# Opening of a linear-attention layer: sums of sizes in place of peaks, another order of the preparations, masks ahead of the bias

## The reference

```python
x = x + attn(layernorm(x))          # qkv = n @ W_attn + b_attn; q, k -> elu(.) + 1
x = x + ffn(layernorm(x))           # x and weight clipped, rounded to e4m3, product in fp16, + bias
def step(carry, inp):               # attention, one token at a time, per head
    kv = kv + kt[..., :, None] * vt[..., None, :]
    ksum = ksum + kt
    num = einsum('bhi,bhij->bhj', qt, kv)
    den = einsum('bhi,bhi->bh', qt, ksum)[..., None] + EPS
    y = num / den                   # then y @ W_proj + b_proj
def _layernorm(x, eps=1e-05):
    return (x - mean) / sqrt(var + eps)
```

## Time and profile before

| what | value |
|---|---|
| median of 3 runs | 1105.98 us (1104.98 to 1107.2) |
| the profiled execution's own time | 1102.66 us |
| its span in the profile | 1100.8 us |
| TensorE, matmuls | 1025.5 us busy, 93% of the span |
| VectorE | 827.4 us, 75% |
| GpSimd | 718.8 us, 65% |
| ScalarE | 568.9 us, 52% |
| granted TensorE clock, mean | 0.992 |

### The profile page before, as it was taken

The page is one execution under the profiler, slowest core; times in us unless marked ns, Lnnn a source line. Parts: engine busy times, 40 slices in busy tenths (PEclk is TensorE's granted clock), DMA queues, the critical chain, the costliest instruction groups (busy, mean ns, idle before and its releaser), DMA issues.

```text
span 1100.8 us, 25183 instructions
## 1 busy us (share of the span) xinstructions
PE 1025.5 (93%) x10112; PEld 557.2 (51%) x10112; DVE 827.4 (75%) x1447; ACT 568.9 (52%) x937; POOL 718.8 (65%) x718
## 2 busy tenths in 40 slices
PE   5877999999999999999999999999999999999976
PEld 2334555555555555555554555555455555555543
DVE  7888767777786867878686786777778777775655
ACT  4454463654646456364555546465554745546343
POOL 5346788576677757667576767758666775864444
PEclk9989999999999999999999999999999999999999
DMA  9201312213131231312213141221313123130011
GB/s 315 39 11 29 78 39 64 59 48 74 42 71 49 59 68 35 87 41 58 63 40 78 45 78 43 60 68 41 73 49 69 43 66 61 40 63 26 25 30 58
DMA packets 121924, 65.59 MB, mean 60 GB/s; under 512 B 102480, under 2 KB 102480, under 8 KB 121808
## 3 DMA queue, kind: packets, MB, share of 16 engines
q1 hardware_dynamic: 121808, 63.99, 23.4%
HBM read 22.81 MB, written 16.78 MB: 36 GB/s over the span
## 4 chain that ended last, share of the span: by engine, by line
PE 41%; POOL 30%; DVE 16%; ACT 6%; issue 6%; DMA 1%; SPq 0%; POOLq 0%; DVEq 0%; ACTq 0%
PE R L219 32%; POOL sm L948 9%; POOL st L916 6%; PE Y L219 5%; POOL xs L964 5%; POOL xn L918 4%; POOL xs L933 4%; DVE st L605 3%; POOL x L918 3%; DVE xs L717 3%; ACT rel L446 2%; PE S L311 2%; ACT qkv L443 2%; DVE state L700 1%; DVE cum L650 1%
## 5 line engine op out<-in xcount | busy, mean ns | idle before, releaser
L219 PE MATMUL R<-xt,wh 128*128 128x512 f16 x960 | 288.1, 382 | 18.2 <-ACT rel L446 17.7
L628 DVE SCALAR_TENSOR_TENSOR qkv<-qkv,rel 128x512 f32<-128x512 f32 x128 | 119.5, 934 | 133.7 <-ACT rel L446 131.9
L916 POOL TENSOR_TENSOR st<-st,half 128x1 f32<-128x1 f32 x128 | 93.4, 730 | 149.1 <-DVE st L610 143.2
L948 POOL TENSOR_SCALAR_AFFINE_SELECT sm<-sm 128x512 f32<-128x512 f32 x184 | 183.4, 1024 | 7.3 <-ACT sm L431 7.3
L219 PE MATMUL R<-xt,wl 128*128 128x512 f16 x480 | 183.0, 381 | 0.0
L219 PEld LDWEIGHTS R<-xt,wh 128*128 128x128 f16 x960 | 89.3, 98 | 124.1 <-ACT rel L446 21.3
L219 PE MATMUL R<-wh,xt 128*128 128x512 f16 x480 | 150.3, 379 | 0.0
L943 POOL TENSOR_TENSOR cum<-cum,qkv 128x512 f32<-128x512 f32 x64 | 84.8, 1325 | 97.6 <-DVE cum L648 50.4
L955 POOL TENSOR_TENSOR yl<-y,yh 128x512 f16<-128x512 f32 x64 | 74.8, 1169 | 97.1 <-ACT yh L431 96.2
L443 ACT ACTIVATE qkv<-R,bqk,wm 128x512 f32<-128x512 f32 x128 | 99.2, 775 | 63.9 <-PE R L219 63.3
L431 ACT ACTIVATE yh<-y 128x512 f16<-128x512 f32 x64 | 40.3, 630 | 155.7 <-DVE y L710 155.7
(11 more groups left out here) (108 smaller groups left out, 1878.8 us busy)
## 6 DMA issues: line engine op xcount, KB each, us to landing
xs<-in_L_attn_x SPq DMA_DIRECT2D x64, 256.0 KB, 2.9
out<-xs SPq DMA_DIRECT2D x64, 256.0 KB, 2.0
qkv<-in_L_attn_W_attn SPq DMA_DIRECT2D x3, 1024.0 KB, 7.9
xs<-in_L_attn_W_proj SPq DMA_DIRECT2D x1, 1024.0 KB, 8.9
rden<-in_L_ffn_weight SPq DMA_DIRECT2D x1, 1024.0 KB, 12.4
x2t<-x2b SPq DMA_TRANSPOSE x62, 2.4
xt<-xnhl SPq DMA_TRANSPOSE x60, 3.2
bv<-in_L_attn_b_attn SPq DMA_DIRECT2D x1, 256.0 KB, 8.1
```

The costliest lines, as they stand in the source:

```text
L219: return e.matmul(out, a, b, start=start, stop=stop, skip_group_check=True)
L628: e.scalar_tensor_tensor(qkv[j % 2][:, i, :], qkv[j % 2][:, i, :], 1.0, rel[:, (u - 1) % 2, :], ALU.min, ALU.add).then_inc(s_phi, 1)
L916: e.tensor_tensor(row[:, 10:11], row[:, 9:10], half[:, :], ALU.pow).then_inc(s_rs, 1)
L948: e.affine_select(out=four(sm[:, h, :]), in_=four(sm[:, h, :]), compare_op=ALU.is_ge, fill=0.0, base=0, pattern=[[0, 4], [1, P]], channel_ ...
```

## The change

Four things change. First, the bounds for the scales of the q, k and projection weights are no longer peaks made by VectorE but sums of absolute values made by ScalarE in one instruction over 128 x 2048 with an accumulated output (`attn_size`, `proj_size`); only the v weight keeps its peak (`v_peak`). The scale of the three is half as large, 2^-14 in place of 2^-13. Second, the lists of the opening are put in another order on all engines, and the fp8 pieces of the feed-forward weight move to the space of `o16` and `x2b`, with one more wait on ScalarE. Third, the negated mean is no longer made; GpSimd subtracts the mean. Fourth, GpSimd masks the scores before it adds the projection's bias, and not behind it.

```diff
-        w_lo = x2[:, 0, :].bitcast(F8)...
-        w_hi = x2[:, 1, :].bitcast(F8)...
+        w_lo = o16[:, :, :]...bitcast(F8)...
+        w_hi = x2b[:, :, :]...bitcast(F8)...
 # TensorE
             def most(i):
-                pe.wait_ge(s_peak, i + 1)
+                if i == 2:
+                    pe.wait_ge(s_peak, 1)
+                else:
+                    pe.wait_ge(s_size, min(i, 2) + 1)
             def k_tokens(n):
                 if n >= 2:
                     pe.wait_ge(s_y, n - 1)
+                elif n:
+                    pe.wait_ge(s_ktok, 1)
-            for m in range(3):
+            for m in range(4):
                 t1(m)
             most(0)
-            t1(3)
             for i in range(12):
                 proj_qkv(0, i)
-                if i in (0, 2):
-                    most(1 if i == 0 else 2)
+                if i in (0, 4, 10):
+                    most((0, 4, 10).index(i) + 1)
             k_tokens(0)
             den(0)
-            most(3)
             for n in range(NT + 2):
...
-                    if c == 0:
+                    if c == 0 and j:
                         lend_out(j, (0, 1))
...
                     ahead(j + 1, 3 * c + 2)
+                    if n == 0:
+                        lend_out(0, (0, 1))
                     if c == 0:
                         lend_out(j, (2, 3))
 # ScalarE
+            def attn_size(i):
+                cols = slice(i * D, (i + 1) * D)
+                act.wait_ge(s_wa[i], 16)
+                e.activation(wl[:, :, cols].bitcast(BF16), raw[:, :, cols], ACT.Abs,
+                             accum_out=wm[:, 7 * i:7 * i + 1]).then_inc(s_size, 1)
+            def proj_size():
+                act.wait_ge(s_wp, 16)
+                e.activation(wpl[:, :, :].bitcast(BF16), raw_p, ACT.Abs, accum_out=wm[:, 21:22]).then_inc(s_size, 1)
...
+            t1(0)
+            t1(1)
+            attn_size(0)
+            t1(2)
+            t1(3)
             attn_weight(0)
             attn_weight(1)
+            attn_size(1)
             phi(0, 0)
             attn_weight(2)
             attn_weight(3)
             phi(0, 1)
             phi(0, 2)
-            attn_weight(4)
             ln1_parts(4)
             phi(0, 3)
-            attn_weight(5)
             ln1_parts(5)
             phi(0, 4)
+            attn_weight(4)
             ln1_parts(6)
             phi(0, 5)
+            attn_weight(5)
             ln1_parts(7)
             phi(0, 6)
+            proj_size()
             phi(0, 7)
...          # in the loop, tile 0: proj_weight() after k_tokens(1), lend_out(0, (0, 1))
...          # after ahead(1, 2), ffn_half() after values(0); t2(n) for n < 2 waits for s_wfd at 5
 # VectorE
-                e.tensor_scalar(row[:, 8:9], row[:, 6:7], -1.0, None, ALU.mult)
...
             for m in range(4):
                 ln1(m)
-            attn_peak(0)
             t1_parts(0)
             t1_parts(1)
+            parts_less()
             scale(0)
             t1_parts(2)
             t1_parts(3)
             attn_weight(0)
             attn_weight(1)
-            attn_peak(1)
             ln1(4)
             scale(1)
+            ln1(5)
             attn_weight(2)
             phi(0, 0)
-            ln1(5)
             attn_weight(3)
             phi(0, 1)
-            attn_peak(2)
+            ln1(6)
             phi(0, 2)
+            v_peak()
+            ln1_parts(4)
+            ln1(7)
+            phi(0, 3)
+            ln1_parts(5)
             scale(2)
-            ...
+            phi(0, 4)
+            denominators(0, 0)
             attn_weight(4)
-            ...
             ln1_parts(6)
             phi(0, 5)
+            denominators(0, 1)
+            attn_weight(5)
+            ln1_parts(7)
             v_scale()
-            ln1_parts(7)
             phi(0, 6)
+            denominators(0, 2)
             phi(0, 7)
-            for g in range(4):
-                denominators(0, g)
-                v_out(0, g)
-            parts_less()
-            proj_peak()
+            denominators(0, 3)
+            for t in range(4):
+                v_out(0, t)
+            ln1(8)
+            proj_scale()
             invert(0)
             den_rest(0)
-            proj_scale()
-            den_third(0)
...          # den_third(0) after scores(0); ffn_low() after update(0), ffn_high() after update(1)
 # GpSimd
-                return e.tensor_scalar(dst, src, row[:, 8:9], row[:, 10:11], ALU.add, ALU.mult)...
+                return e.tensor_scalar(dst, src, row[:, 6:7], row[:, 10:11], ALU.subtract, ALU.mult)...
...
                     if n + 8 < NT:
                         ln1(n + 8)
-                        add_bp(n + 8)
                     scores(n)
                     after(j + 1, 3 * c)
+                    if n + 8 < NT:
+                        add_bp(n + 8)
 # SyncE
-                if n == 0:
+                if n == 1:
                     sp.wait_ge(s_wfd, 5)
                     for f in range(4):
                         e.dma_start(wft[:, :, f * P:(f + 1) * P], w_b[:, f, :], transpose=True)...
```

More of the change, by code:

```diff
@@ L164, in build @@
         s_xth, s_wh, s_relu, s_whi = sem("xth"), sem("wh"), sem("relu"), sem("whi")
-        s_xhi, s_ktok, s_dene = sem("xhi"), sem("ktok"), sem("dene")
+        s_xhi, s_ktok, s_dene, s_size = sem("xhi"), sem("ktok"), sem("dene"), sem("size")
         s_top16, s_mid16, s_rden = sem("top16"), sem("mid16"), sem("rden")
@@ L523, in t2 @@
                     act.wait_ge(s_x2t[i], 16 * (n // 2))
+                else:
+                    act.wait_ge(s_wfd, 5)
                 copy(x2b[:, i, :], x28[:, :]).then_inc(s_x2b, 1)
@@ L543, in ahead, with t1 @@
                         den(j)
-            for m in range(4):
+            def t1(m):
                 act.wait_ge(s_t1, m + 1)
                 copy(xt0[:, 0:4, m * P:(m + 1) * P], four(bank["t1", m][:, :])).then_inc(s_xth, 1)
+            t1(0)
[3 more added lines that the diff above has]
+            t1(3)
             attn_weight(0)
             attn_weight(1)
+            attn_size(1)
             phi(0, 0)
@@ L576, in _ @@
                         ln1_parts(n + 8)
-                    if n == 0:
-                        proj_weight()
                     ahead(j + 1, 3 * c + 1)
-                    if c == 0:
+                    if c == 0 and j:
                         lend_out(j, (0, 1))
@@ L583, in _ @@
                     k_tokens(n + 1)
+                if n == 0:
+                    proj_weight()
                 if n >= 2:
@@ L587, in _ @@
                     ahead(j + 1, 3 * c + 2)
+                    if n == 0:
+                        lend_out(0, (0, 1))
                     if c == 0:
                         lend_out(j, (2, 3))
-                    if n == 0:
-                        ffn_half()
                     if c == 3 and j + 1 < NB:
@@ L594, in _ @@
                     values(n)
+                if n == 0:
+                    ffn_half()
                 if n >= 2:
@@ L754, in scale @@
                 dve.wait_ge(s_range, 3 * i + 2)
-                e.tensor_scalar(wm[:, at + 4:at + 5], wm[:, at + 3:at + 4], 2.0 ** -13, None,
+                e.tensor_scalar(wm[:, at + 4:at + 5], wm[:, at + 3:at + 4], 2.0 ** (-13 if i == 2 else -14), None,
                                 ALU.mult).then_inc(s_range, 1)
@@ L758, in scale, with v_peak @@
                 e.reciprocal(wm[:, at + 5:at + 6], wm[:, at + 4:at + 5]).then_inc(s_up, 1)
-            def attn_peak(i):
-                dve.wait_ge(s_wa[i], 16)
-                peak(raw[:, :, i * D:(i + 1) * D], wm[:, 7 * i:7 * i + 1], AX.XY).then_inc(s_peak, 1)
+            def v_peak():
+                dve.wait_ge(s_wa[2], 16)
+                peak(raw[:, :, 2 * D:], wm[:, 14:15], AX.XY).then_inc(s_peak, 1)
             def t1_parts(m):
@@ L791, in v_scale @@
                 e.tensor_scalar(bv[:, :], bv[:, :], wm[:, 32:33], None, ALU.mult).then_inc(s_bv, 1)
-            def proj_peak():
-                dve.wait_ge(s_wp, 16)
-                peak(raw_p, wm[:, 21:22], AX.XY).then_inc(s_peak, 1)
             def proj_scale():
@@ L878, in _ @@
                 if n < NT:
-                    if n + 8 < NT:
+                    if n and n + 8 < NT:
                         ln1(n + 8)
                     scores(n)
+                    if n == 0:
+                        den_third(0)
                     ahead(j + 1, 3 * c)
@@ L886, in _ @@
                         ln1_parts(n + 8)
-                    if n == 0:
-                        ffn_low()
                     ahead(j + 1, 3 * c + 1)
@@ L897, in _ @@
                     ahead(j + 1, 3 * c + 2)
-                    if n == 0:
-                        ffn_high()
                     values(n)
                     update(n)
+                    if n == 0:
+                        ffn_low()
+                    if n == 1:
+                        ffn_high()
                     if c == 3 and j + 1 < NB:
@@ L917, in norm @@
```

(2 more changed lines are left out.)

11 lines of the change are left out of this document (2 added, 9 removed).

## The result

The changed kernel takes 1234.48 us (1233.57 to 1235.28, four runs) against 1106.09 us; the ratio is 1.116 with a 95% interval of 1.1141 to 1.118. It is 128.4 us slower; 1080 was forecast, with a range to 1091. The profiled execution took 1233.57 us, its span is 1231.7 us.

A forecast was written before the change was run, and what follows sets the result against it. TensorE was taken as the bound, so only its 75.3 us of idle time could shrink. Opening 9.8, masks 14.9 and norms 1.3 sum to 26.0 us, from 1105.98 to 1080 us; range 1073 to 1091.

The forecast's parts named there:

- the part on the norms: All 128 norms: one small VectorE instruction less each, GpSimd's norm still one instruction, nothing lost there; 1.3 us gained.
- the slower rival: Middle: masks now beside VectorE's two-input work cost 1.36 us a tile, half on TensorE's path; 1118 us, chance 0.03.
- Masks: Middle: masks ahead of the bias add end 1.5 us earlier, removing TensorE's 26 waits for `sm`; 14.9 us, bounds 5 to 14.9.
- The doubt that another partner would take them back: Middle: the next late partner replaces the masks' waits, 5 us of 14.9 left; 1090 us, chance 0.10.
- Norms without negated means: VectorE's statistics: 0.07 us less per norm, shortening 14 waits for `rel` and the last four norms; 1.3 us, bounds 0 to 2.5.
- Opening: Start to the scores of tile 3: reordered preparations bring these from 119.81 to 110.0; 9.8 us gained, bounds 4 to 13.
- The walk: Opening followed on TensorE step by step: gains of 3.8, 6.8 and 13.0 us, partly given back in tile 2, leaving 9.8.
- rival (a): Opening gives little: `ffn_high` keeps VectorE late, or the sixth low weight's wait lowers the clock; 1086 to 1088 us, chance 0.17.
- the third term: The 1.3 us gained by no longer making the negated mean for the norms on VectorE.
- The sum over 128x2048: Opening, ScalarE: absolute values with a sum in one instruction, taken as 2.0 us, between 1.8 and 4.8.
- rival (c): Opening, ScalarE: table loads on both sides of each sum, six of 1.28 us, some 4 on the path; 1084 us, chance 0.06.
- so I count no slow stretch: Opening, new 2.9 us stall before the first product of v: clock expected to hold, as behind an earlier 2.76 us wait.

The follow-up runs named there:

- the run with the pieces moved: Changed kernel with the old add-and-multiply norm, and the five pieces of the feed-forward weight's rounding moved into idle time in tile 0: 1068.71 us, ratio 0.9663.
- the run with the forms: Kernel before, with another pair of operations in GpSimd's norms by tile modulo 8 (most tiles compute other values): 1151.5 us.
- the reordered kernel: Changed kernel with old norm and feed-forward pieces moved into idle time, plus parts_less, scale(2), late weights and running sums reordered in the opening: 1066.17 us, ratio 0.9639.

## Why the prediction was wrong

**The step that failed** is in the part on the norms: "Nothing is lost on GpSimd, whose norm stays one instruction." The count was right, but no row showed that the duration would stay. The trace of before shows add+mult on 128x512 at 767 ns and no subtract in that form. I gave the new pair the price of the old one and set no bounds on it from both sides. The trace of before held a warning: a two-input add over the same shape takes 1.28 us on average there (the second bias add), so GpSimd's time depends on more than size. Subtract+mult costs 2.08 us, 128 x 1.31 = 168 us of GpSimd, and on the path of TensorE 155.9 us (1234.48 - 1078.58). No rival named the norm; the slower rival (masks shut out by VectorE) named the wrong mechanism.

**Masks.** Right in direction and cause: no wait for `sm` from 100 to 1050 us was left with the masks moved alone or with the old norm; in the changed kernel 5.7 us in 14 are, behind the slow norms. The term was 14.9 us and measured 26.3, in the main because the table of waits counts from the modelled end of the last matmul. The doubt that another partner would take them back was unfounded, as were the 38 us of the slower rival.

**Norms without negated means.** Priced at 1.3 us for the VectorE instruction less; the kernel that adds the mean is 4.7 us under the one with the old norm (one run against a median of four). Only VectorE's own 0.07 us was counted, and not what came with it: the wait of 1.28 us in every second block fell to 0.72.

**Opening.** 9.8 us forecast, 3.4 measured alone and 0.6 beside the masks (1079.21 - 1078.58, inside the scatter; in the traces tile 4 starts within 0.6 us of where it started without the new opening). The walk was right for GpSimd's `part` holding `scale(0)` (forecast 14.1, 13.97 in the run with the old norm), for the first product (16.4 and 16.30), for the stall that goes and for the wait of 4.5 us in `lend_out` (5.6 in three). Too small were the wait for the sixth low weight (2.9, measured 4.55, with the clock at 0.66 from 45 to 50, where I had it hold) and that of tile 2 (4, measured 6.59, with clock 0.51 behind it). This is rival (a), which the run with the pieces moved bears out. For opening and masks together 24.7 us were forecast and 26.9 measured: a gain of the opening that was put too high and one of the masks that was put too low nearly cancel. With the third term and a norm of the old price, 26.0 were forecast and 31.7 measured (1105.52 - 1073.86, the run that adds the mean). That the total without the slow pair came out near 1080 is luck.

**The sum over 128x2048** was priced at 2.0 us. The groups of ScalarE after (count | busy, mean ns):

```profile
L458 ACT ACTIVATE wl<-qkv 128x2048 bf16<-128x2048 f32 x2 | 3.8, 1898 | 0.0
...
L436 ACT ACT_TABLE_LOAD x1 | 1.3, 1283 | 0.8 <-PEq L1135 0.8
...
L458 ACT ACTIVATION_READ_ACCUMULATOR wl<-qkv 128x1 f32 x2 | 0.4, 190 | 0.0
```

It is 1.90 us and 0.19 for reading the accumulator. There is one table load in the whole trace, at the start as before, so rival (c) is out. The Trainium skill (ScalarE: Activation LUTs, Table sets) says that abs stands in every set; the trace agrees for the one set that this kernel loads, whose exp runs beside it.

## What to carry to other kernels

A rewrite that saves an instruction by another pair of operations is a new instruction: until a trace shows that pair on that engine and shape, its price is open, and where it stands twice in a chain that already ends waits, each microsecond more can be two in each tile (here 1.31 more was 2.8). Time it alone first. Read TensorE's waits as a lower bound where short matmuls overlap, and take their price from the distance between two fixed points of a tile in a kernel with and without them.

## What the runs showed of the hardware

- GpSimd's `tensor_scalar` with two scalars over 128x512 fp32, in the run with the forms: 0.77 us for add+mult, mult+add, mult+mult and min+max; 2.08 us for subtract+mult, mult+subtract, add+subtract and subtract+add; 1.57 us for add or subtract alone.
- A subtract of two tensors on GpSimd is not slow: 1.17 us on average for y's low part (fp16 out), against 1.28 for the second bias add, in the trace of before.
- TensorE's granted clock stayed at its upper level behind 2.76 us of idle time in the kernel before (1.00 from 90.3 to 96.0 us) and fell behind 4.55 us (0.66 from 45 to 50 us) and behind 6.59 us (0.51 from 111 to 117). But the length of one wait doesn't settle it: in the changed kernel it fell behind the 2.38 us of the tile shown (0.50 from 569 to 571 us), and in the reordered kernel behind 2.73 us (0.57 from 89 to 92). The forecast's "so I count no slow stretch" can't be carried over from one wait to another.
